# Group 0's q projected into repeated rows on chip, and three V projections moved into the first attention pass

## The reference

```python
x = x + xattn(layernorm(x), ctx)      # x (1, 1024, 128), ctx (1, 6404, 96)
x = x + ffn(layernorm(x))             # main MLP, and 2 of 8 experts by a gate
# xattn, 16 heads of 8 columns
q, k, v = query @ Wq + bq, ctx @ Wk + bk, ctx @ Wv + bv
attn = softmax(clip(q @ k.T * 8**-0.5, -1e4, 1e4))
x = (attn @ v) @ Wo + bo
```

## Time and profile before

| what | value |
|---|---|
| median of 3 runs | 792.22 us (791.56 to 793.74) |
| the profiled execution | 791.66 us, span 789.6 us |
| mean granted clock of TensorE | 0.994 |
| busy PE / ACT / DVE / POOL | 93% / 91% / 71% / 4% of the span |
| chain that ended last | PE 56%, ACT 20%, issue 17%, DVE 3%, DMA 3% |

### The profile page before, as it was taken

The page is one execution under the profiler, slowest core; times in us unless marked ns, Lnnn a source line. Parts: engine busy times, 40 slices in busy tenths (PEclk is TensorE's granted clock), DMA queues, the critical chain, the costliest instruction groups (busy, mean ns, idle before and its releaser), DMA issues.

```text
span 789.6 us, 13262 instructions
## 1 busy us (share of the span) xinstructions
PE 731.2 (93%) x5406; PEld 217.3 (28%) x5406; DVE 557.9 (71%) x776; ACT 717.9 (91%) x572; POOL 31.6 (4%) x54
## 2 busy tenths in 40 slices
PE   6889989999999999999989999999999999999798
PEld 3524322222222222222222222222222222222457
DVE  5924358798878978797788897897889782139320
ACT  4578999999999999999999999999999999999351
POOL 5710000000000000000000000000000000000000
PEclk9979999999999999999999999999999999999999
DMA  5856300011110000111100000111100000000010
GB/s 165 254 151 185 99 1 1 18 43 43 34 34 1 1 1 2 34 37 48 51 1 2 1 1 18 36 44 40 35 1 1 1 1 1 2 0 2 2 54 27
DMA packets 19132, 29.06 MB, mean 37 GB/s; under 512 B 6247, under 2 KB 9693, under 8 KB 19069
## 3 DMA queue, kind: packets, MB, share of 16 engines
q1 hardware_dynamic: 12730, 23.71, 10.1%
q0 software_dynamic: 5120, 3.83, 1.9%
q10 hardware_dynamic: 1218, 0.64, 0.3%
HBM read 20.02 MB, written 8.13 MB: 36 GB/s over the span
## 4 chain that ended last, share of the span: by engine, by line
PE 56%; ACT 20%; issue 17%; DVE 3%; DMA 3%; POOL 0%; POOLq 0%; SPq 0%; ACTq 0%
PE po L1189 30%; PE ps L1104 17%; ACT region_ctx L522 14%; ACT probs_own L522 5%; PE ps L1281 2%; PE po L1291 1%; DMA qst<-q_dram 1%; PE po L1009 1%; PE po L1175 1%; DMA q_dram<-dres 1%; PE po L1104 1%; DMA xres<-in_x 1%; PE po L1084 1%; DMA region_ctx<-in_w1e 0%; PE ps L1291 0%
## 5 line engine op out<-in xcount | busy, mean ns | idle before, releaser
L522 ACT ACTIVATE region_ctx<-ps 128x1536 f32<-128x1536 f32 x375 | 528.7, 1511 | 8.2 <-PE ps L1104 8.0
L1189 PE MATMUL po<-region_ctx,v 128*9 128x512 f32 x2238 | 390.9, 596 | 0.5 <-ACT region_ctx L522 0.5
L1104 PE MATMUL ps<-qst,region_k 32*128 32x512 f32 x1492 | 252.9, 496 | 40.4 <-ACT region_ctx L522 26.0
L1104 PEld LDWEIGHTS ps<-qst,region_k 32*128 32x128 f32 x1492 | 96.7, 182 | 413.0 <-ACT region_ctx L522 288.3
L522 ACT ACTIVATE probs_own<-ps 128x1536 f32<-128x1536 f32 x125 | 188.9, 1511 | 6.7 <-PE ps L1104 6.3
L1189 PE MATMUL po<-probs_own,v 128*9 128x512 f32 x746 | 192.9, 598 | 0.0
L805 DVE TENSOR_SCALAR region_kT<-po 128x512 f32<-128x512 f32 x108 | 74.1, 687 | 98.3 <-PE po L1104 98.3
L808 DVE SCALAR_TENSOR_TENSOR region_kT<-region_kT,po 128x512 f32<-128x512 f32 x108 | 73.6, 681 | 0.3
L844 DVE SCALAR_TENSOR_TENSOR dres<-region_kT,dres 128x1024 f32<-128x1024 f32 x54 | 66.1, 1225 | 1.7
L841 DVE SCALAR_TENSOR_TENSOR dres<-region_kT,dres 128x1024 f32<-128x1024 f32 x54 | 65.8, 1219 | 0.2
L835 DVE SCALAR_TENSOR_TENSOR region_kT<-region_kT 128x1024 f32<-128x1024 f32 x54 | 65.8, 1219 | 0.0
(11 more groups left out here) (203 smaller groups left out, 324.4 us busy)
## 6 DMA issues: line engine op xcount, KB each, us to landing
region_k<-k_dram SPq DMA_DIRECT2D x40, 320.0 KB, 3.3
k_dram<-kparts SPq DMA_DIRECT2D x18, 320.0 KB, 3.5
qst<-q_dram POOLq DMA_DIRECT2D x16, 128.0 KB, 9.1
region_ctx<-in_ctx SPq DMA_DIRECT2D x2, 624.0 KB, 9.1
q_dram<-dres POOLq DMA_DIRECT2D x2, 512.0 KB, 4.6
k_dram<-kparts SPq DMA_DIRECT2D x2, 322.0 KB, 3.3
region_ctx<-in_ctx SPq DMA_DIRECT2D x1, 576.0 KB, 7.5
xres<-in_x SPq DMA_DIRECT2D x1, 512.0 KB, 4.3
```

The costliest lines, as they stand in the source:

```text
L522: act.activation(probs_of(t), ps[t % NSB][:, :], ACT.Exp, scale=ESCALE).then_inc(exp_ready, 1)
L1104: return mm(dst, kst[r, kt * P:(kt + 1) * P], qst[r, g, queries], start=True, stop=True)
L1189: last = mm(dst[QUAD * j:QUAD * j + V9, :], w, src, start=first, stop=last_one, skip_group_check=True)
```

## The change

Group 0's q no longer passes through DRAM. DVE makes `wq_rep`, which has each of the 32 columns of Wq of group 0 in its repeated places, and `pick`, the same of the identity, with which a small matmul repeats the bias (`brep`). PE projects `qrep` with `wq_rep` where it projected q before, ACT evicts it to float32 rows, and DVE (`pick_q`) rounds them to `qhi` and writes to `qst[:, 0]` the rounded value in rows for the first part and the rest in rows for the second. The plain q is projected one chunk of K later, and is split (`split_q`) and stored behind the last reductions of K; POOL loads groups 1 to 3 from it. |q| is taken behind the last reduction of K. POOL writes the ones in `v9` ahead of the q stores.

V's chunks 0 and 1 are projected behind the first score tile, chunks 2 to 4 as spare jobs at tiles 2, 5 and 8, and every later chunk six tiles later than before (chunk c at 3c - 4), up to tile 32. The splits of K segments 4 to 9 hang on V's chunks 2 to 7 in place of 5 to 10.

```diff
-V_AT = {c: 3 * c - 10 for c in range(VPRE, VCH)}
-BOUND_TILES, GSUM_TILE, ROWS_TILE = (3, 6), 9, 12
+V_AT = {c: 3 * c - 4 for c in range(2, VCH)}
+BOUND_TILES, GSUM_TILE, ROWS_TILE = (3, 7), 10, 12
...
-SPLIT_BEHIND = {SPARE.index((V_AT[c], "v", c)): s for c, s in zip(range(VPRE, VCH), range(4, NSEG))}
+SPLIT_BEHIND = {SPARE.index((V_AT[c], "v", c)): s for c, s in zip(range(2, VCH), range(4, NSEG))}
...
+            pool.wait_ge(pads_ready, 3)
+            pool.memset(v9[:, :, :, D:V9], 1.0).then_inc(vones_ready, 1)
             for b in range(PARTS):
                 pool.wait_ge(qparts_ready, b + 1)
                 pool.dma_start(q_dram[:, :, b, :], qparts[:, b, :].bitcast(F32)).then_inc(qparts_stored, 16)
             pool.wait_ge(qparts_stored, 16 * PARTS)
-            load_q(pool, 0)
-            pool.wait_ge(pads_ready, 3)
-            pool.memset(v9[:, :, :, D:V9], 1.0).then_inc(vones_ready, 1)
...
             evac_k(act, 3)
+            act.wait_ge(brep_ready, 1)
+            for n in range(NHALF):
+                act.wait_ge(qrep_psum, n + 1)
+                act.activation(qrep[:, n * BANK:(n + 1) * BANK], po[n][:, :], ACT.Identity, bias=rowc[:, 2:3], scale=QSCALE).then_inc(qrep_ready, 1)
+            evac_ctxT(act, 5)
+            evac_k(act, 4)
             act.wait_ge(bqs_ready, 1)
...
+            dve.wait_ge(const_ready, 3)
+            rows4 = [t[:, :].rearrange("c (j a d r) -> c j a d r", j=GH, a=PARTS, d=D) for t in (wq_rep, pick)]
+            for t, from_ in zip(rows4, (wq_sb, ident)):
+                heads = from_[:, 0:GH * D].rearrange("c (j d) -> c j d", j=GH).unsqueeze(3).broadcast_to([C, GH, D, PARTS])
+                for a in range(PARTS):
+                    last = v.tensor_copy(t[:, :, a, :, :], heads)
+            last.then_inc(pick_ready, 1)
+            link(v.tensor_reduce(rowc[:, 0:1], ident[:, :].rearrange("p (n r) -> p r n", r=PARTS)[:, 1, :], AX.X, ALU.add))
+            link(v.tensor_scalar(rowc[:, 1:2], rowc[:, 0:1], -2.0, 1.0, ALU.mult, ALU.add))
...
+            def pick_q(n):
+
+                cols = slice(n * BANK, (n + 1) * BANK)
+                dve.wait_ge(qrep_ready, n + 1)
+                link(v.tensor_copy(qhi[:, cols], qrep[:, cols]))
+                link(v.tensor_scalar(qrep[:, cols], qrep[:, cols], rowc[:, 0:1], None, ALU.mult))
+                v.scalar_tensor_tensor(qst[:, 0, cols], qhi[:, cols].bitcast(F32), rowc[:, 1:2], qrep[:, cols],
+                                       ALU.mult, ALU.add).then_inc(q0_ready, 1)
...
                 if c == 3:
-                    split_q()
-                if c == 5:
-                    link(v.scalar_tensor_tensor(q_abs, qT[:, :], -1.0, qT[:, :], ALU.mult, ALU.max))
+                    pick_q(0)
+                if c == 6:
+                    pick_q(1)
                 if c in (4, 7, 9):
                     split_k(1 + (4, 7, 9).index(c), link)
-                if c >= KCH - 1 - VPRE:
-                    dve.wait_ge(v_psum, c - (KCH - 1 - VPRE) + 1)
-                    take_v(c - (KCH - 1 - VPRE), po[(c - (KCH - 1 - VPRE)) % 2]).then_inc(v_done, 1)
...
             last.then_inc(tailT_ready, 1)
+            dve.wait_ge(v_psum, 1)
+            take_v(0, po[0]).then_inc(v_done, 1)
             link(range_k(KCH - 1))
+            dve.wait_ge(q_ready, NHALF)
+            link(v.scalar_tensor_tensor(q_abs, qT[:, :], -1.0, qT[:, :], ALU.mult, ALU.max))
...
+            dve.wait_ge(v_psum, 2)
+            take_v(1, po[1]).then_inc(v_done, 1)
...
+            split_q()
...
+            pe.wait_ge(pick_ready, 1)
+            mm(bank(2, P, 1), pick[:, :], bqc[:, :], start=True, stop=True).then_inc(brep_psum, 1)
             ctx_transpose(4)
             project_k(3)
             pe.wait_ge(wts_in, 48)
             for n in range(NHALF):
                 pe.wait_ge(xnT_ready, n + 1)
+                mm(po[n][:, :], wq_rep[:, :], xnT[:, n * BANK:(n + 1) * BANK], start=True, stop=True).then_inc(qrep_psum, 1)
+            pe.wait_ge(brep_ready, 1)
+            ctx_transpose(5)
+            project_k(4)
+            for n in range(NHALF):
+                pe.wait_ge(qrep_ready, n + 1)
                 mm(po[n][:, :], wq_sb[:, :], xnT[:, n * BANK:(n + 1) * BANK], start=True, stop=True).then_inc(q_psum, 1)
...
-                n = c - (KCH - 1 - VPRE)
-                if 0 <= n < VPRE:
...
-                    project_v(n, po[n % 2]).then_inc(v_psum, 1)
...
+                    if g == 0:
+                        pe.wait_ge(q0_ready, half + 1)
+                    else:
+                        pe.wait_ge(qst_in[g], 16 * GH)
...
             score_tile(0)
+            pe.wait_ge(q_ready, NHALF)
+            project_v(0, po[0]).then_inc(v_psum, 1)
+            project_v(1, po[1]).then_inc(v_psum, 1)
             pe.wait_ge(k_ready, KCH)
             score_tile(1)
```

More of the change, by code:

```diff
@@ L57 @@
 NPRE = 14
-VPRE = 5
-V_AT = {c: 3 * c - 10 for c in range(VPRE, VCH)}
-BOUND_TILES, GSUM_TILE, ROWS_TILE = (3, 6), 9, 12
+V_AT = {c: 3 * c - 4 for c in range(2, VCH)}
+BOUND_TILES, GSUM_TILE, ROWS_TILE = (3, 7), 10, 12
 CB = HID // P
@@ L251, in build @@
         qparts = dres[:, 0, 0:PARTS * NQ].bitcast(F32R).rearrange("p (a n) -> p a n", a=PARTS)
+        qrep = dres[:, 1, 0:NQ]
+        qhi = dres[:, 1, NQ:2 * NQ].bitcast(F32R)
+        rowc = sb("rowc", [P, 4])
         vtail = sb("vtail", [P, NG, P])
@@ L281, in build @@
         pT = sb("pT", [P, 2, P])
+        wq_rep, pick = qm, pT[0:C, 0, :]
         gen = sb("gen", [P, 8])
@@ L313, in build @@
         qst_in = [sem(f"qst_in{g}") for g in range(NG)]
+        pick_ready, brep_psum, brep_ready = sem("pick_ready"), sem("brep_psum"), sem("brep_ready")
+        qrep_psum, qrep_ready, q0_ready = sem("qrep_psum"), sem("qrep_ready"), sem("q0_ready")
         ktail_in, ktail_ready = sem("ktail_in"), sem("ktail_ready")
@@ L416, in _ @@
                     sp.wait_ge(kst_in[s], 16)
-                for g in range(NG):
+                for g in range(1, NG):
                     sp.wait_ge(qst_in[g], 16 * GH)
@@ L510, in _ @@
                                accum_out=ksum[:, KCH + n:KCH + n + 1]).then_inc(q_ready, 1)
-            for c in range(4, KCH):
+            for c in range(5, KCH):
                 if c + 1 < KCH:
@@ L649, in _ @@
                 v.tensor_copy(xnT[:, n * BANK:(n + 1) * BANK], po[n][:, :]).then_inc(xnT_ready, 1)
+            dve.wait_ge(brep_psum, 1)
+            v.tensor_scalar(rowc[:, 2:3], bank(2, P, 1), QSCALE, None, ALU.mult).then_inc(brep_ready, 1)
             dve.wait_ge(wts_in, 48)
@@ L1091, in scores @@
                 queries = slice(half * BANK, (half + 1) * BANK)
-                if ("q", g) not in seen:
-                    seen.add(("q", g))
-                    pe.wait_ge(qst_in[g], 16 * GH)
+                if ("q", g, half) not in seen:
+                    seen.add(("q", g, half))
+                    if g == 0:
+                        pe.wait_ge(q0_ready, half + 1)
+                    else:
+                        pe.wait_ge(qst_in[g], 16 * GH)
                 if kt == FULL:
@@ L1117, in spare_job @@
                 t, kind, i = SPARE[n]
-                pe.wait_ge(v_done, VPRE)
+                pe.wait_ge(v_done, 2)
                 if n:
```

## The result

The changed kernel takes 788.92 us (median of 20 runs, 787.27 to 794.5) against 793.04 for the kernel before beside it (20 runs, 791.56 to 795.01). The ratio is 0.9951, with a 95% interval of 0.994 to 0.9961: 3.9 us faster by the ratio (the medians differ by 4.1), where 4.5 was forecast. The forecast time was 787.7, and 788.92 lies in its range of 785.3 to 791.5. The execution that was profiled is one of the slower ones: 791.65 us, span 789.7, mean granted clock 0.991, as long as the profiled execution of the kernel before (791.66).

What follows compares the result with a forecast made beforehand. The prediction took PE's wait for group 0's q to set the start, then mostly PE's pace up to tile 28; -6.6 + 0.9 + 1.2 = -4.5 gave 787.7 us on the median, range 785.3 to 791.5.

Steps and rivals of the forecast that it cites:

- the prediction's own sign: Around the first tiles: granted clock 1.00 from 35 to 50; prediction wrong if a stretch there is near 0.5.
- Term 1: Start of the attention: first exponential at 35.1 us against 41.71, -6.6 us.
- V's second copy: DVE's work ahead of the first value step: sum of 17.8 us from 23.0, ending at 40.8.
- The clock pays for that: First eight tiles: clock stays up without idle stretches over about 1.5 us, paying for three more V projections.
- Rival C: First tiles: clock falls all the same, ten microseconds at half clock give back 5.0; +0.5, 792.7 us; chance 0.09.
- Term 2: First eight tiles, to tile 8's exponential: 14.4 us against 13.49, +0.9 us.
- tiles 8 to 28: Stretch of the first pass with the same jobs at the same tiles: no difference.
- Term 3: Tiles 29 and 32 get V jobs that were not there: 0.6 us each, +1.2 us.
- No segment is late: First pass: K splits, stores and loads come behind V jobs three tiles earlier, and no K segment is late.
- Rival D: POOL holds both picks, V's second copy comes near 48.4: slower, +3.1, 795.3 us; chance 0.05.
- E: Start: scores wait for the K segment or another load until about 38.5; -0.2, 792 us; chance 0.05.

Runs made afterwards that it cites:

- the second execution: The changed kernel, unaltered, profiled a second time: 785.46 us, clock 1.00 in every stretch on record; that session's median 789.38 us (7 runs).
- memset_late_v: v_order with POOL's memset of the row of ones waiting for DVE's first K split; 784.09 us, 0.9887 of the kernel before.
- v_order: Changed kernel with V's chunks 0 and 1 projected behind the second score tile and V's second copy ahead of |q| and bounds; 785.34 us.
- behind_only: Changed kernel with only V's chunks 0 and 1 projected behind the second score tile, V's second copy unmoved; 789.93 us, 0.9952 of before.
- q_only: Changed kernel with V's chunks 0 to 4 kept between K projections and later ones at old tiles; 790.6 us, 0.9967 of before.
- v_spread_v: v_order with V's chunks 2 to 12 mostly at tiles without a value step, small rows' job at tile 13; 785.82 us, 0.9912 of before.
- v_only: Kernel before with V moved as in the change, group 0's q still through DRAM; 800.1 us, 1.0084 of before.
- copy_only: Changed kernel with only V's second copy on DVE moved ahead of |q| and the bounds; 786.65 us, 0.9924 of before.
- qload_late_v: v_order with POOL's loads of q for groups 1 to 3 held until the last K split; 785.0 us, 0.9903 of before.

## Why the prediction was right, and where it was not

The time, the sign and the first term were right; one step failed, and it was nearly made up for by errors the other way. That 788.92 came so near to 787.7 is luck in part. At full clock the changed kernel has 785.5, 2.2 under the forecast, and its commonest clock costs it 3.6 (789.1). By the prediction's own sign it would be wrong: a stretch there has a clock near 0.5 in the profiled execution. The base moved too, from 792.22 (3 runs) to 793.04 (20 runs).

- **The start.** Term 1 was -6.6. Measured -6.63 and, in the second execution, -6.93. The first was 0.3 late as a whole, so the second is the one to compare. Its parts, forecast and then measured in the second and the first execution: the repeated q projection 0.8 later than 19.01 (0.61, 0.90), chunk 6's transposes at 24.6 (24.43, 24.72), the first scores at 34.2 (34.17, 34.46). That the memset would hold DVE was right; that all of the copies would stand behind it was not, since two ran before it. memset_late_v shows the cause: without the memset beside them all four copies took 0.28 a pair. The rule on the locked port pair, from the page "SBUF — State Buffer" of the Trainium skill (SBUF: two separate sides), agrees with the trace: the copies ahead of the memset took 0.29, those that met it 5.61. They start within 0.01 us of the memset, so the trace can't tell which of the two is to be called the first.
- **V's second copy.** Forecast for 40.8, measured 40.1 (39.43 + 0.68), 39.8 in the second execution. The first pick was held 1.2 us by the ones' memset (1.66 against 0.42 for the second pick's CAST), for which I had 1.5. PE's gap ahead of the first value step was 0.74 in the execution at full clock, not 1.3.
- **The failed step: "The clock pays for that: PE has no idle stretch over about 1.5 us, and was at 1.00 in 16 to 25.5 with 1.26 of waiting".** The first gap was foreseen at about 1.0 (1.41 measured), its effect was not. One stretch without a fall was taken for a bound, and the trace of before spoke against it: in its long wait, which began at 37.5, the clock was down from 39.3 on, less than two microseconds in. Of the 27 runs 26 lost some of the upper clock, most 0.004 of the mean, which is 3.1 us of time (0.004 x 787); v_order shows that closing the gaps brings it back, and behind_only that it stays away where one gap is closed and the other grows to 2.17; in q_only it fell behind two gaps under 1.0. Rival C was priced rightly per episode (5.0, measured 4.2) and given 0.09: it should have been a part of the forecast, with a shorter episode.
- **At full clock the sum was too small.** -4.5 was forecast; the execution at 1.00 gives -6.2 against the profiled one of before (785.46, 791.66). Term 2 was +0.9, measured +0.69; tiles 8 to 28, put at nothing, gave -0.47 (32.48 against 32.95); with term 1's 0.3 that makes 1.0 of the 1.7. Another 0.54 comes after tile 44, little by little within the attention: tile 44 is 5.56 earlier than before (104.29 against 109.85), tile 497 6.14 (722.68 against 728.82). What changes there was not looked into.
- **Term 3.** +1.2; measured 22.85 against 21.70 from tile 28 to tile 44: +1.15. The price of 0.6 per job, between the 0.5 and the 1.09 of before's own stretches, held. v_spread_v shows it to be a property of the stretch and not of the tile.
- **K's segments.** "No segment is late" held for the scores, but not for DVE: a split waited 1.72 us for the buffer's store in the first execution. It cost 0.6 us there: tiles 8 to 28 take 33.07, and 32.48 in the second execution, which has no such wait.
- **Rival D and E** did not come. v_only is a harder case than E, with scores from 43.5 in place of 38.5: with q from DRAM the moved V jobs are a loss of 6.7.

What stays open is why one execution keeps its clock over a gap of 1.4 us and the next doesn't, and why the tiles behind tile 44 each come a little sooner.

## What to carry to other kernels

Price a gap on TensorE twice: for itself, and for what a fall of the clock behind it costs; where PE is the bound, a reordering that shortens a gap of one or two microseconds can be worth more than the work that it moves. Look at the mean granted clock of every run before a difference is explained, since here two executions of one program differed by 6 us. And move work past a wait only together with what removes the wait: V's part alone cost 6.7 us, with q's part it was a gain.

## What the runs showed of the hardware

- The granted clock went from its upper level (2.4 GHz) to its lower (1.2 GHz) behind a single gap of 1.41 us in copy_only and behind two of 0.91 and 0.93 in q_only, and stayed up over 1.41 and 0.74 in the second execution of the changed kernel. In its first execution it fell once more in the middle of the steady part (0.87 in 390 to 400 us), behind a wait of PE's of 1.32 us for DVE.
- Once down, the clock stayed down while PE was busy: PE worked for all of the 6.75 us from 38.95 to 45.7 in copy_only, at 0.50.
- A gap filled with matmuls that nobody reads kept the clock as long as they ran (1.00 up to 43.2), but two gaps of 1.21 and 1.33 us followed it, and the clock fell.
- At the kernel's start the matmuls run slower than later: two of the K projection take 2.07 us at 11.35 and 1.02 at 18.26 in the first execution.
- A memset of one row of 6432 numbers on POOL held copies on DVE that take 0.28 us for 5.6.
- A store of K that lands in 3.3 us alone (qload_late_v) took up to 10.5 beside POOL's twelve q loads.
